# Edge stage of a graph layer: TensorE's program written as loops of six batches, node rows copied to fixed buffers by ScalarE, three gather buffers without the landing pause, relu first in ScalarE's turn

## The reference

```
xn  = layernorm(x)
msg = relu(xn[src] + edge_attr)                 # 106,250 x 256
agg = zeros_like(xn).at[dst].add(msg)           # the edge stage
h   = bn(( xn + agg) @ W1 + b1); gnn = xn + graph_norms(relu(h) @ W2 + b2)
q, k, v = split(xn @ W_qkv + b_qkv)             # centred over channels
k2  = k*k / sum(k*k); k2 = k2 / norm over nodes # keys: sums over all nodes
q2  = q*q / sum(q*q); q2 = q2 / norm over channels
mix = (v + q2 @ (k2.T @ v) / sqrt(N)) @ W_out + b_out
x   = x + gnn + mix
x   = x + mixture_of_experts(layernorm(x))      # 8 experts, top 2
```

## Time and profile before

| | |
|---|---|
| median of 3 runs | 2415.05 us (2396.78 to 2415.8) |
| the profiled execution | 2420.91 us |
| span in the profile (first to last instruction) | 2419.3 us, 34,670 instructions |
| TensorE busy | 1818.1 us (75%) |
| VectorE busy | 1260.5 us (52%) |
| GpSimd busy | 1178.5 us (49%) |
| ScalarE busy | 795.5 us (33%) |
| DMA bytes | 356.62 MB, mean 147 GB/s |
| edge stage in the trace | first gather at 70.8 us, last window sum at 1368 us |

### The profile page before, as it was taken

The page is one execution under the profiler, slowest core; times in us unless marked ns, Lnnn a source line. Parts: engine busy times, 40 slices in busy tenths (PEclk is TensorE's granted clock), DMA queues, the critical chain, the costliest instruction groups (busy, mean ns, idle before and its releaser), DMA issues. The chain is left out here.

```text
span 2419.3 us, 34670 instructions
## 1 busy us (share of the span) xinstructions
PE 1818.1 (75%) x10022; PEld 1444.7 (60%) x10023; DVE 1260.5 (52%) x3894; ACT 795.5 (33%) x1606; POOL 1178.5 (49%) x1121
## 2 busy tenths in 40 slices
PE   3365666656657776777677698968479999999996
PEld 3243554444544444445444487857368888888885
DVE  7454555555545545455455376655944444444442
ACT  4122222222212222222222156855034444444442
POOL 1576666776766665656666100022034444444443
PEclk8588778788778777888888799955789999999998
DMA  7555556565545555555555354646713322232222
GB/s 238 175 191 178 183 187 204 169 209 183 193 160 196 182 169 188 191 182 188 185 193 195 97 168 167 230 139 188 289 32 46 49 44 44 46 48 46 44 45 34
DMA packets 142044, 356.62 MB, mean 147 GB/s; under 512 B 33130, under 2 KB 79625, under 8 KB 127611
## 3 DMA queue, kind: packets, MB, share of 16 engines
q0 software_dynamic: 66624, 157.12, 25.0%
q1 hardware_dynamic: 69068, 198.31, 23.2%
q10 hardware_dynamic: 6255, 0.10, 0.3%
HBM read 297.49 MB, written 57.94 MB: 147 GB/s over the span
## 5 line engine op out<-in xcount | busy, mean ns | idle before, releaser
L190 POOL DMA_INDIRECT gathered<-xn_rows,src_table x832 | 843.9, 1014 | 431.9 <-issue 250.9
L795 PE MATMUL bank<-edge_attr,dst_select 128*128 128x256 f32 x1664 | 553.4, 504 | 393.5 <-ACT edge_attr L723 209.5
L795 PEld LDWEIGHTS bank<-edge_attr,dst_select 128*128 128x128 f32 x1664 | 425.8, 263 | 518.7 <-ACT edge_attr L723 230.0
L1783 PE MATMUL bank<-rowsT_parts,expert_weights 128*128 128x256 f16 x3564 | 409.3, 274 | 10.1 <-issue 6.3
L614 DVE TENSOR_SCALAR dst_select<-iota_window,dst_partition 128x128 f32<-128x128 f32 x832 | 257.0, 310 | 288.0 <-DMA gathered<-xn_rows,src_table 235.3
L1783 PEld LDWEIGHTS bank<-rowsT_parts,expert_weights 128*128 x3564 | 346.8, 98 | 59.0 <-issue 18.1
L723 ACT ACTIVATE edge_attr<-edge_attr 128x2048 f32<-128x2048 f32 x104 | 198.3, 1906 | 457.2 <-DVE edge_attr L625 312.8
L625 DVE TENSOR_TENSOR edge_attr<-gathered,edge_attr 128x256 f32<-128x256 f32 x832 | 344.1, 414 | 0.0
L1744 POOL DMA_INDIRECT out<-expert_out,output_row_of_slot x108 | 183.1, 1696 | 301.1 <-ACTq L1842 278.6
L1889 DVE SCALAR_TENSOR_TENSOR gated<-bank,silu 128x512 f32<-128x512 f32 x216 | 120.6, 558 | 184.9 <-ACT silu L1828 173.7
L635 DVE SCALAR_TENSOR_TENSOR node_sum<-bank,in_first_tile,node_sum 128x256 f32 x104 | 49.8, 479 | 308.7 <-PE bank L795 173.6
(11 more groups left out here) (273 smaller groups left out, 1978.4 us busy)
## 6 DMA issues: line engine op xcount, KB each, us to landing
edge_attr<-in_edge_attr SPq DMA_DIRECT2D x104, 1024.0 KB
raw_weights<-in_L_ffn_w SPq DMA_DIRECT2D x32, 544.0 KB, 4.6
expert_weight_parts<-weight_parts SPq DMA_DIRECT2D x32, 544.0 KB, 3.1
expert_weights<-expert_weight_parts SPq DMA_DIRECT2D x8, 2176.0 KB, 25.5
gathered<-xn_rows,src_table POOLq DMA_INDIRECT x832
rows_in<-xn_rows SPq DMA_DIRECT2D x48, 128.0 KB
rows_in<-in_x SPq DMA_DIRECT2D x48, 128.0 KB
residual_rows<-residual_tile SPq DMA_DIRECT2D x48, 128.0 KB
```

The source lines that it names most:

```text
L190: pool.indirect_dma_start(out=k.GA[h][:, e, :], out_offset=None, in_=k.xn_d[:, :], in_offset=bass.IndirectOffsetOnAxis(ap=k.src[:, b, e:e ...
L795: last = pe.matmul(WINP[b % 2][:, 0:C], SEL[b % 3][:, e, :], EA[b % 3][:, e, :], start=e == 0, stop=e == EK - 1)
L1783: last = pe.matmul(bank[:, jj * TT:(jj + 1) * TT], w(e, wp, at + b * step, 128), X16[h][:, xp, b, :], start=n == 0, stop=n == 3 * CB - 1)
```

## The change

Of the edge stage alone:

- TensorE's program: batches 0 to 5, 48 to 59, 102 and 103 stay written out; 6 to 47 and 60 to 101 become two hardware loops of 7 rounds each, with six batches in the body (six is a multiple of the 2 and the 3 buffers). Inside a loop each semaphore wait compares with a value worked out from the loop's register.
- A loop's body needs fixed operand addresses, so the tile's columns of `xnT` are copied by ScalarE into one of two fixed buffers `XS` (`rowsT`, 98 copies of 128x256 float32), one batch ahead. TensorE waits for `xs_done` before `keys` and `query_value`.
- Gather buffers: three instead of two (`AHEAD`), GpSimd waits until batch b-3 is added; the landing pause is gone. Memory for it comes from reusing key buffers for the queries and from `w_out`, which moves to the layernorm stage's own memory.
- ScalarE's turn begins with the relu; the rest follows in the old order.
- VectorE adds the window of batch b-2 (`LATER`) instead of b-1 into the node sums, and TensorE's scatter waits for that (`evac`).

```diff
-def gather(k, pool, b, h):
+def gather(k, pool, b, rows, done):
     for e in range(EK):
-        pool.indirect_dma_start(out=k.GA[h][:, e, :], ...).then_inc(k.g_in[h], 16)
+        pool.indirect_dma_start(out=rows[:, e, :], ...).then_inc(done, 16)
...
-    GA, g_in = k.GA, k.g_in
+    GA = [*k.GA, sb("gathered2", [128, EK, C], F32, st)]
+    g_in = [*k.g_in, sem("gathered_in2")]
...
-    Q2 = [sb(f"query_squared{h}", [128, C], F32, st) for h in two]
-    Q4 = sb("query_fourth", [128, C], F32, st)
-    Q2T = [sb(f"query_squaredT{h}", [128, CB, NP], F32, st) for h in two]
+    Q2, Q4 = K2[0:2], K2[2]
+    Q2T = [K4[h][:, :].rearrange("p (b n) -> p b n", b=CB) for h in two]
...
-    RT = [sb(f"residual_tile{h}", [128, C], F32, st) for h in two]
+    RT = KB
+    XS = [sb(f"node_rowsT{h}", [128, CB, NP], F32, st) for h in two]
...
             for b in range(1, NB):
-                if b % RUN == 0:
-                    pool.wait_ge(g_in[(b - 1) % 2], 16 * EK * ((b - 1) // 2 + 1))
-                if b >= 2:
-                    pool.wait_ge(added, b - 1)
-                gather(k, pool, b, b % 2)
+                if b >= AHEAD:
+                    pool.wait_ge(added, b - AHEAD + 1)
+                gather(k, pool, b, GA[b % AHEAD], g_in[b % AHEAD])
...
                 add(b)
-                if b > 0:
-                    into_tiles(b - 1)
+                if b >= LATER:
+                    into_tiles(b - LATER)
...
+            def rowsT(n):
+                if n >= 2:
+                    if n - 2 < PT:
+                        act.wait_ge(kp_full, n - 1)
+                    else:
+                        act.wait_ge(qv_full, n - 1 - PT)
+                v = rows_of(n % PT)
+                act.activation(XS[n % 2][:, :, 0:v], k.XNT[:, n % PT, :, 0:v], ACT.Copy).then_inc(xs_done, 1)
+
             for b in range(NB):
+                relu(b)
+                if is_tile(b + 1 - P1):
+                    rowsT(b + 1 - P1)
+                if is_tile(b + 1 - P2):
+                    rowsT(b + 1 - P2 + PT)
                 if is_tile(b - P2 - 1):
                     query_fourth(b - P2 - 1)
                     query_turned(b - P2 - 1)
-                relu(b)
-                if is_tile(b - P2 - 1):
                     query_norm(b - P2 - 1)
...
-            def scatter(b):
+            def scatter(b, j):
+                if not first_two(b):
+                    pe.wait_ge(evac, b - LATER + 1)
                 pe.wait_ge(relu_done, b + 1)
...
+            for b in range(SIX):
+                turn(b)
+            with pe.Fori(1, KEY_END // SIX) as i:
+                for j in range(SIX):
+                    b = i * SIX + j
+                    keys(b - P1, j - P1, NP)
+                    key_sums(b - P1 - 2, j - P1 - 2, NP, False, False)
+                    scatter(b, j)
+            for b in range(KEY_END, ASK_BEGIN):
+                turn(b)
+            with pe.Fori(ASK_BEGIN // SIX, ASK_END // SIX) as i:
+                for j in range(SIX):
+                    b = i * SIX + j
+                    query_value(b - P2, j - P2, NP)
+                    query_turns(b - P2 - 1, j - P2 - 1, NP)
+                    scatter(b, j)
+                    mixed(b - P2 - 1, j - P2 - 1, NP)
+            for b in range(ASK_END, NB):
+                turn(b)
```

More of the change, by code:

```diff
@@ L184, in rows_of @@
     return min(NP, N - t * NP)
[L187 removed]
+def gather(k, pool, b, rows, done):
     for e in range(EK):
[L190 to L191 removed]
+        pool.indirect_dma_start(out=rows[:, e, :], out_offset=None, in_=k.xn_d[:, :],
+                                in_offset=bass.IndirectOffsetOnAxis(ap=k.src[:, b, e:e + 1], axis=0)).then_inc(done, 16)
 def layernorm_stage(k, st):
@@ L227, in layernorm_stage @@
     rw = sb("router_w", [NX, C], F32, st)
+    k.wout = sb("w_out", [128, CB, C], F32, st)
     x_in = [sem(f"x_in_{h}") for h in range(NX_BUF)]
@@ L333, in _ @@
             pool.wait_ge(xn_st, 16 * (NG + 1))
-            gather(k, pool, 0, 0)
+            gather(k, pool, 0, k.GA[0], k.g_in[0])
         @block.vector
@@ L714, in _ @@
                     finish_keys()
-            into_tiles(NB - 1)
+            for b in range(NB - LATER, NB):
+                into_tiles(b)
             for t in range(NB - P2 - 2, PT):
@@ L828, in key_weights, with query_value, query_turns @@
                 last.then_inc(kw_full, 1)
-            def query_value(t):
-                v = rows_of(t)
-                if t == 0:
+            def query_value(t, j, v):
+                if the_first(t):
                     pe.wait_ge(kw_ready, 1)
-                if t >= 3:
+                if not (isinstance(t, int) and t < 3):
                     pe.wait_ge(r_done, t - 2)
+                pe.wait_ge(xs_done, t + PT + 1)
                 for c in range(CB):
[L837 to L841, removed]
+                    pe.matmul(QV[j % 3][0:v, :], XS[(j + PT) % 2][:, c, 0:v], k.wqv[:, c, :], start=c == 0, stop=False)
+                pe.matmul(QV[j % 3][0:v, :], k.ones[0:1, 0:v], k.brow[0:1, :], start=False, stop=True).then_inc(qv_full, 1)
+            def query_turns(t, j, v):
+                h = j % 2
                 pe.wait_ge(q2_done, t + 1)
@@ L845, in query_turns, with mixed @@
                 last.then_inc(qt_full, 1)
-            def mixed(t):
-                v, h = rows_of(t), t % 2
+            def mixed(t, j, v):
+                h = j % 2
                 pe.wait_ge(q2t_done, t + 1)
-                if t == 0:
+                if the_first(t):
                     pe.wait_ge(stray_out, 1)
@@ L854, in mixed, with turn @@
                 last.then_inc(t_full, 1)
[L856 to L864, removed]
+            def turn(b):
+                for t, work in ((b - P1, keys), (b - P1 - 2, key_sums), (b - P2, query_value), (b - P2 - 1, query_turns)):
+                    if is_tile(t):
+                        work(t, t, rows_of(t), *((t == 0, t == PT - 1) if work == key_sums else ()))
                 if b == FIN:
                     key_weights()
-                scatter(b)
-                if is_tile(b - P2 - 1):
-                    mixed(b - P2 - 1)
+                scatter(b, b)
+                t = b - P2 - 1
+                if is_tile(t):
+                    mixed(t, t, rows_of(t))
+            for b in range(SIX):
[17 more added lines that the diff above has]
+                turn(b)
             for t in range(NB - P2 - 1, PT):
-                query_turns(t)
-                mixed(t)
+                query_turns(t, t, rows_of(t))
+                mixed(t, t, rows_of(t))
 def stray_stage(k, st):
```

29 lines of the change are left out of this document (17 added, 12 removed).

## The result

The changed kernel takes 2451.7 us in the median of 4 runs (2447.76 to 2453.8), the one before 2412.01 (2396.78 to 2415.8) beside it: a ratio of 1.0187, 95% interval [1.0154, 1.0219]. It is slower by 1.9%, where 6% faster was forecast, and the time lies outside the range.

A forecast was written before the change was run, and what follows sets the result against it. GpSimd's gathers were taken to bound the first pass, a ScalarE-TensorE ring the second. Gathers 145.8 plus tail 12 minus remainder 12 saved 146 us from 2420.9: 2275 profiled, median 2269, range 2248 to 2352.

The forecast's parts named there:

- the ten late copies: ScalarE's copies in the second pass, read as waiting for TensorE's code; loops would remove up to 53 us, not added.
- 145.8: Edge-stage gathers: without landing waits and most add waits, the last gather ends 145.8 us earlier, at 1196.6.
- The slack is 15 us against any disturbance: Edge-stage gather buffers: three free a buffer 15 us before GpSimd wants it, against 4.5 with two.
- Late windows stay: Rival: VectorE's 79 us of remote idle lands on the gathers' floor, as scatter waits for the window; 2348 us, 12%.
- The slower rival: DMA queues are never left alone, so 40 code packets hold engines 5.8 us each, 232 us; 2500 us, 10%.
- The remainder of 12 us: Edge-stage time not absorbed (batch 52's chain, late windows, TensorE catching up): 12 us lost, between 0 and 30.
- the tail: Last gather to last window at the edge stage's end: 26 us falls to about 14, 12 less.
- 2269: Predicted median for the whole kernel, from 2275 for the profiled execution, which is 5.9 above the median.
- TensorE's register waits at zero: Waits in TensorE's loops cost nothing; the rival at 0.76 us each, 59 us in all, gave 2328 us, 12%.
- ScalarE's copies of node rows: New edge-stage copies at 0.50 us each, beside other work; 49 us if that cover were gone.
- such stall: Rival: each turn of TensorE's loops fetches its code again, 30 us in all; 2299 us, 8%.
- a ring: Second pass: ScalarE and TensorE wait on each other, 12.6 us per batch; relu first opens it, leaving gathers at 10.8.

The follow-up runs named there:

- e3: Kernel before with relu first in ScalarE's turn alone, on chip 0: 2371.1 us, ratio 1.0017 to the kernel before.
- e1: Changed kernel with the landing pause put back ahead of every even batch, on chip 0: 2350.0 us, ratio 0.9928 to the kernel before.
- f1: Changed kernel with TensorE's program written out straight and the pause every second batch, on chip 15: 2351.9 us, ratio 0.9928 to the kernel before.
- e2: Kernel before with only the landing pause taken out, two buffers kept, on chip 0: 2299.5 us, ratio 0.9717 to the kernel before.
- e4: Changed kernel with TensorE's program written out straight, fixed waits, on chip 0: 2258.6 us, ratio 0.9542 to the kernel before.
- the four stretches: Changed kernel with batches 26-51 paused, 52-77 gathering 64-channel rows, 78-103 loading an eighth of the edge attributes, on chip 13: 2444.2 us (one run).

## Why the prediction was wrong

**The step that failed** is the reading of the ten late copies: "I read the late copies as TensorE's code arriving". I had one coincidence, ten packets and ten copies, and didn't look at what the other engines did at 1067.13. GpSimd had just stopped. From the wrong cause came the wrong sign: I expected the lateness to go with the loops, and so took the pause as pure cost, 94.7 us of waits to be saved, while it was what kept the lateness short. The last gather was to end at 1196.6 us, 145.8 earlier than before; it ended at 1366.0, 23.6 later.

**"The slack is 15 us against any disturbance"** is right as a size and fell with that step. A disturbance of 5.75 us, as in the earlier trace rows, would have been absorbed. This one grows with the row of gathers, and without the pause the rows are up to 48 long with three buffers. Here the holds reach 31 us, against 15.

**"Late windows stay", 2348, 12%** counted 79 of the 211 us of "remote" and kept them constant. They went to 780 when the thing that bounded them was removed.

**The slower rival, 2500, 10%**, had the sign and the place (the pause is the moment at which others get through) but another mechanism, DMA queues never left alone. The DMA share did not rise here (0.55 and 0.58), and where it did, to 0.62 on chip 11, nothing was late. The stretches with a third less on the DMA engines had the most holds. Its chance was put too low: it was the only case that asked what the pause did for anybody else.

**Right, where no hold occurs.** On chip 11 the terms can be checked one by one: gathers end at 1189.8 (1196.6 forecast), busy 862.4 (853), idle 260.5 (273). From there to the last window sum it is 16.4 us against 25.9 before, so the tail is 9.5 less where 12 was forecast. The remainder of 12 us did not appear at all: the last gather ended 6.8 us earlier than the sum without it. Relus are 10.8 and 10.7 us apart (10.7 to 10.9). The forecast of 2275 for the profiled execution was 17 too high. But that 2269 is near 2260 is partly luck. The gain there is 108 us, not 146: these chips start from 2367, and e3, 4 us from the kernel before there, shows no holds. My guess is that part of the 145.8 was holds, which those chips never had; no trace of the kernel before was taken on one of them.

**TensorE's register waits at zero** held: e1 against f1. ScalarE's copies of node rows took 0.40 us, where 0.5 was put. The page "Runtime: NRT & Kernel Launch" of the Trainium skill, section "Instruction fetch mechanics", says that a taken branch out of the current window stalls. The looped kernel is not measurably slower than the straight one on chip 6 (2468 and 2461 us, intervals overlapping) nor with the pause on chips 0 and 15, so no such stall shows here.

**Relu first** opens a ring that was not the bound on a chip without holds: alone it is worth nothing there (1.0017). The 12.6 us per batch that I read as that ring included the late copies. On a chip with holds it wasn't tried alone. e2 shows that taking the pause away alone gives 2.8% on a chip without holds, with two buffers; the rest of e4's 4.6% is the third buffer, relu first and the later window together, which were not tried apart on top of it.

**Left open.** Why a long row of gathers holds the others up, and only on some chips; each chip was met once, so it could be the chip or its condition then. Whether the pause would make the changed kernel faster than before on such a chip: its one stretch went at 11.8 us, the kernel before at 11.7 in the same batches, so a gain would have to come from the second pass (12.8 before), where no pause was tried, and no whole kernel with the pause ran there. What the third buffer and relu first do on such a chip without each other is open as well. Whether a memset would do.

## What to carry to other kernels

Before a pause or a wait is taken out, look at what other engines do in it: if late starts on several engines end in or right after it, it may be serving them. A wait put down to "remote" that sits near another engine's stop is a question, and a count that happens to match is no answer. And when an edit and the chip change together, measure the edit's parent again: here the kernel before told, by 2367 or 2431 us, which kind of chip the ratio was from.

## What was not expected of the hardware

- Chips differ. The kernel before took 2367, 2368, 2367, 2369 and 2361 us on chips 0, 15, 11, 7 and 9, but 2431 on chip 6 and 2415 on chip 13, and the same change gave 0.955 on chip 11 and 1.014 on chip 6. No trace on the first kind has a hold, five of them of versions of the changed kernel with no stop of GpSimd added (looped, straight, with fewer bytes, with the memset). On the second kind every trace has them: four of the changed kernel, looped or straight, that of the four stretches, and both of the kernel before. The chip of the first measurement is of the second kind.
- During a hold what TensorE has finished reaches SyncE, ScalarE and VectorE up to 31 us late, and what VectorE has finished reaches ScalarE up to 6.6 us late. It mostly starts at the 10th to 18th gather in an unbroken row of one each 1.25 us. Deep in a long row TensorE does one instruction in 1.40 us: 62 times in the trace of the changed kernel, from the 17th gather on and mostly past the 28th, and not once in the first trace of the kernel before. The page "SBUF — State Buffer" of the Trainium skill, section "Who interferes with whom", has VectorE and GpSimd alone contend for a port, and TensorE and ScalarE wait for nobody; a port lock of that kind doesn't explain these traces, since TensorE and SyncE are slowed too.
- A `drain` on GpSimd behind gathers costs 2.9 us of idle time, more than waiting for them to land (medians of 2.05 to 2.55 us in eight traces).
